# One of the four sums of x made by an accumulating transfer in a two-layer LoRA kernel

## The reference, cut to what matters

```python
base_out = jnp.einsum('bti,oi->bto', x, W) + b
lora_h = jnp.einsum('bti,bir->btr', x, A)
lora_out = jnp.einsum('btr,bro->bto', lora_h, Bm)
return base_out + lora_out * SCALING
...
x = x + _L0_cond_ref(x, itok_B_0_23, L0_cond_W, L0_cond_b, L0_cond_lora_As, L0_cond_lora_Bs)
x = x + _L1_cond_ref(x, itok_B_6_15, L1_cond_base_weight, L1_cond_base_bias, L1_cond_lora_A_w, L1_cond_lora_B_w)
```

## Time and profile before

| what | us |
|---|---|
| median of three runs (310.71 to 312.2) | 311.84 |
| the profiled execution, its own time | 312.06 |
| its span, first to last instruction | 310.5 |
| TensorE matmul, busy | 303.0 (98%) |
| VectorE, busy | 194.5 (63%) |
| ScalarE, busy | 90.3 (29%) |
| GpSimd, busy | 18.6 (6%) |

### The profile page before, as it was taken

How to read it: one execution, slowest core, us unless ns; L and a number is a source line. 1 busy time by engine, 2 the same in 40 slices (tenths; PEclk the granted TensorE clock), 3 DMA queues, 4 the chain that set the end, 5 groups by cost and what they waited for, 6 DMA issues and landing times.

```text
span 310.5 us, 4006 instructions
## 1 busy us (share of the span) xinstructions
PE 303.0 (98%) x1427; PEld 250.1 (81%) x1427; DVE 194.5 (63%) x328; ACT 90.3 (29%) x144; POOL 18.6 (6%) x43
## 2 busy tenths in 40 slices
PE   6999999999999999998999999999999999999995
PEld 4788898888887488886888888888888888888884
DVE  4777624994749362188897676487486485585312
ACT  4555534012122302293224223232231322232000
POOL 2233240000000010000000000000000000000000
PEclk9999999999999999999999999999999999999999
DMA  6996150000000055504054360440631711602002
GB/s 205 383 372 243 36 183 21 0 0 2 0 0 3 17 179 209 164 1 135 0 193 140 121 179 34 153 146 34 202 128 42 223 62 70 219 36 84 19 34 101
DMA packets 14744, 33.94 MB, mean 109 GB/s; under 512 B 2149, under 2 KB 2277, under 8 KB 14726
## 3 DMA queue, kind: packets, MB, share of 16 engines
q1 hardware_dynamic: 13702, 31.60, 30.0%
q0 software_dynamic: 1024, 2.10, 2.2%
HBM read 22.09 MB, written 11.60 MB: 109 GB/s over the span
## 4 chain that ended last, share of the span: by engine, by line
PE 91%; DVE 4%; ACT 2%; DMA 1%; SPq 0%; issue 0%
PE bank L807 28%; PE bank L921 16%; PE bank L920 16%; PE bank L922 16%; PE bank L940 4%; PE bank L819 3%; PE bank L927 2%; DMA stage<-W 1%; PE bank L895 1%; PE bank L897 1%; PE bank L896 1%; PE bank L821 1%; DVE w L602 1%; PE bank L868 1%; PE bank L906 1%; PE bank L907 1%
## 5 line engine op out<-in xcount | busy, mean ns | idle before, releaser
L807 PE MATMUL bank<-w,w_hi 128*128 128x512 f32 x256 | 80.9, 401 | 0.8 <-ACT w L350 0.6
L807 PEld LDWEIGHTS bank<-w,w_hi 128*128 128x128 f32 x256 | 49.2, 194 | 13.1 <-ACT w L350 1.3
L807 PE MATMUL bank<-w,w_lo 128*128 128x512 f32 x128 | 49.0, 390 | 0.0
L407 ACT CAST xa<-xr 128x512 fp32r<-128x512 f32 x32 | 19.6, 621 | 33.6 <-PE bank L927 17.3
L807 PEld LDWEIGHTS bank<-w,w_lo 128*128 128x128 f32 x128 | 24.1, 188 | 5.1
L921 PE MATMUL bank<-w_lo,w 128*128 128x512 f32 x64 | 25.1, 392 | 0.0
L922 PE MATMUL bank<-w_hi,w 128*128 128x512 f32 x64 | 25.1, 392 | 0.0
L920 PE MATMUL bank<-w_hi,w 128*128 128x512 f32 x64 | 25.0, 391 | 0.0
L921 PE MATMUL bank<-w 128*128 128x512 f32 x64 | 25.0, 391 | 0.0
L920 PE MATMUL bank<-w 128*128 128x512 f32 x64 | 25.0, 391 | 0.0
L920 PE MATMUL bank<-w_hi,xa 128*128 128x512 f32 x64 | 25.0, 390 | 0.0
(11 more groups left out here) (127 smaller groups left out, 493.4 us busy)
## 6 DMA issues: line engine op xcount, KB each, us to landing
xr<-xT SPq DMA_DIRECT2D x32, 256.0 KB, 4.2
out<-stage SPq DMA_DIRECT2D x28, 256.0 KB, 2.0
stage<-W SPq DMA_DIRECT2D x7, 512.0 KB, 5.0
stage<-W1T SPq DMA_DIRECT2D x7, 512.0 KB, 5.9
a<-rb_rows SPq DMA_DIRECT2D x8, 392.0 KB
rb_rows<-a SPq DMA_DIRECT2D x3, 512.0 KB
rb_rows<-b0w SPq DMA_DIRECT2D x3, 512.0 KB
out<-rows SPq DMA_DIRECT2D x4, 256.0 KB, 2.7
```

The lines of the kernel that those rows point to most:

```text
L407: nc.scalar.copy(x_op(j, 0), raw(j)).then_inc(op_hi[j], 1)
L807: return mm(d_bank(m, h)[:, :], left[:, m, k * P:(k + 1) * P], right[:, k, h * HALF:(h + 1) * HALF], start=start, stop=stop)
```

## The change

For batches 1 to 7 VectorE no longer makes S1. SyncE loads A21 a second time, straight into the tile of S1 (256 KB, right behind the ordinary load of A21), and GpSimd's queue then adds A22 from DRAM to it with an accumulating transfer (256 KB). ScalarE's `high_x(S1, b)` and VectorE's `sum_s2(b)` wait for that transfer (`s1_summed`) instead of VectorE's own sum. Batch 0 keeps the sum on VectorE. `load_a0(b)` for b from 2 on now alternates with the accumulating transfers on GpSimd's queue.

```diff
@@ load_x
-                        for s in {A11: (S2, S3), A21: (S1, S3), A12: (S4,), A22: (S1,)}[j]:
+                        for s in {A11: (S2, S3), A21: (S3,), A12: (S4,), A22: ()}[j]:
                             sp.wait_ge(s_made[s], b)
+                        if b == 1 and j in (A21, A22):
+                            sp.wait_ge(s_made[S1], 1)
                         if j in (A21, A12):
                             sp.wait_ge(op_lo[S3 if j == A21 else S4], b)
                     sp.dma_start(xr[:, j, :], xT[b, :, j, :]).then_inc(x_landed[j], DMA)
+                    if j == A21 and b >= 1:
+
+                        sp.wait_ge(op_lo[S1], b)
+                        sp.wait_ge(s_made[S2], b)
+                        sp.dma_start(s_raw[S1], xT[b, :, A21, :]).then_inc(s1_first, DMA)
@@ gpsimd
-            for b in range(2, B):
-                load_a0(b)
+            for b in range(1, B):
+                if b >= 2:
+                    load_a0(b)
+                pool.wait_ge(s1_first, b * DMA)
+                pool.dma_start(s_raw[S1], xT[b, :, A22, :], accum_op=ALU.add).then_inc(s1_summed, DMA)
@@ scalar, high_x
+                elif j == S1 and b >= 1:
+                    act.wait_ge(s1_summed, b * DMA)
@@ vector
             def sum_s1(b):
+                if b >= 1:
+                    return
                 dve.wait_ge(x_landed[A21], (b + 1) * DMA)
                 dve.wait_ge(x_landed[A22], (b + 1) * DMA)
-                if b >= 1:
-                    dve.wait_ge(op_lo[S1], b)
                 nc.vector.tensor_tensor(s_raw[S1], xr[:, A21, :], xr[:, A22, :], ALU.add).then_inc(s_made[S1], 1)
 
             def sum_s2(b):
...
-                dve.wait_ge(s_made[S1], b + 1)
+                if b >= 1:
+                    dve.wait_ge(s1_summed, b * DMA)
+                else:
+                    dve.wait_ge(s_made[S1], 1)
```

More of the change, by code:

```diff
@@ L180, in lora_pair @@
         op_lo = [sem(f"op_lo{j}") for j in range(8)]
+        s1_first = sem("s1_first")
+        s1_summed = sem("s1_summed")
         s_made = {j: sem(f"s_made{j}") for j in (S1, S2, S3, S4)}
```

## The result

The changed kernel takes 316.65 us (median of four, 315.62 to 318.16) against 311.64 us for the kernel before (median of four here, 310.71 to 312.2; its 311.84 above is of three of these), a ratio of 1.017 with a 95% interval of 1.011 to 1.0225. It is slower by 5.0 us; 3.1 of it is one wait of TensorE, in the place that was foretold. The trace is of the slowest of the four executions, 318.16 us.

The account below looks back on a forecast made before the run. TensorE, busy for 98% of the span, was taken as the bound. A 1.9 us stall in batch 2 and 0 us for all else, added to the median of 311.84, gave 313.7 us; range 311.2 to 320.7.

Parts of the forecast that it names:

- L: GpSimd's accumulating transfer, time from issue to landing: taken as 4.5 us, between 2.5 and 7.0 us.
- the sum: The forecast's addition over the batches: 1.9 us of TensorE stall in batch 2, 0 us elsewhere.
- the case that came true: The prediction's own case: L from 4.15 to 6.3 us, one stall in batch 2; chance 0.44.
- VectorE's relief: Batches 1 to 7: seven sums, 4.8 us busy time, leave VectorE; covered by TensorE's products, worth 0 us.
- Batch 2 is the tightest: Batch 2, prepared during batch 1: slack before TensorE needs u4 is 0.8 us, so it stalls 1.9 us.
- the hand-over: From the S1 copy's landing on SyncE to GpSimd's start of the accumulating transfer: taken as 0.3 us.
- rival 2: Slow transfer, L above 6.3 us: batches 3 to 7 stall too, 320.7 us at L = 7.0; chance 0.17.
- Rival 1: Quick transfer, L from 2.5 to 4.15 us: batch 2 stalls 0 to 1.55 us, no measurable change; chance 0.36.
- Now the S1 copy has this place: SyncE's loads in batch 2: the copy, third in order, issued at 160.5, lands 3.7 us later, at 164.2.
- the formula: Batch 2's stall: S2 starts at 164.6 + L, latest allowed 167.2, so TensorE waits L - 2.6 us.
- Batches 1 and 3 to 7: The chain fits up to L = 6.0 in batch 1 and 6.3 in batches 3 to 7: 0 us.
- The other loads at 0 us: SyncE's A12, A22 and factor loads and stores go 0.45 us later, their readers come later still: 0 us.

## Why the prediction was right, and where it was too small

The measured 316.65 us lies in the range (311.2 to 320.7) and on the forecast side; the forecast of 313.7 was 3 us too low. That the range holds it is in part luck: it was drawn so wide for an L of up to 7.0 us, L was 4.3, and what used up the room was not in the sum. The range of the case that came true, 313.4 to 315.8, was missed by 0.8 us.

- **VectorE's relief is worth nothing: right.** 5.8 us less busy time (foretold 4.8), no gain, also where the chain was harmless.
- **Batch 2 is the tightest, and `fill_z(1)` waits for u4: right**, in place and in number (once), but for 3.1 us in place of 1.9. With the start's 1.2 us taken off, the copy's issue (160.5), the hand-over (0.3 us), the 0.1 us to VectorE and the 4.6 us from S2 to u4 are those of the sum.
- **L = 4.5 us: near.** It was 4.3 us, well under rival 2's 6.3. Its terms came out as 3.5 us for the plain transfer in batch 2 (in the sum 3.6 + 0.2) and 0.8 us for the add (0.7), the latter from one execution of each kernel. Rival 1's bound of 4.15 us was only 0.1 us off: with the copy as foretold, the stall would have been 4.3 - 2.6 = 1.7 us, just above its 1.55. The estimate of 2.6 us from the Trainium skill, "DMA: Bandwidth & Descriptors", is under every transfer measured, with the add (4.0 to 5.0) or without (3.5 to 5.3).
- **"Now the S1 copy has this place", landing after 3.7 us: this is the step that failed.** I took the landing time of the load that had held third place. The copy needed 5.6 us, 1.9 more. The added load was priced as if it queued, not as something that changes the landing of those beside it; the runs show that its source being read twice and the load of A22 behind it both add, 0.9 us each, taken one at a time. With 5.6 and 4.3 the formula gives 160.5 + 5.6 + 0.3 + 4.3 + 0.1 - 167.2 = 3.6 us, the 3.5 us measured.
- **The clock was not in the sum.** 1.2 us of the loss is matmuls at the lower level behind the standstill. I had read a clock of full tenths in all slices and priced a stall by its length.
- **Batches 1 and 3 to 7: right, but barely for batch 3.** There the copy took 6.3 us and the transfer 5.0; the chain from the copy's issue to S2 was 6.3 + 0.3 + 5.0 + 0.1 = 11.7 us, where the sum leaves room for 189.2 - 177.6 = 11.6. `fill_z(2)`'s weight load waited 0.2 us and no matmul did, where 1.8 us had been foretold as left over. Batch 1's S2 waited 0.6 us on VectorE, covered.
- **The other loads at 0 us: nearly right.** The sum let only the loads behind the copy go later. But A21's load ahead of it landed 1.0 us later in batch 2 (4.3 us in place of 3.3 from issue), and the weight load behind u2 waited 0.3 us; the slack there hid all but 0.2 us.

## What to carry to other kernels

Work taken off an engine that isn't waited for is worth nothing, while the transfers that replace it must fit the slack of the tightest pass, which here was the first full one and not the average one. A transfer put among others in flight made them land later here, so neither its old neighbour's landing time nor an earlier start can be counted in full: hold back the transfers that nobody needs yet. A stall of TensorE of 2 to 3 us should be priced with something on top for the clock, here 1.2 to 1.5 us in five of seven traces.

## What was not expected of the hardware

- Loads in flight hold each other up: with a fifth 256 KB load and the accumulating transfer, the x loads' median from issue to landing went from 4.2 to 5.4 us; the accumulating transfer took 4.3 us behind the loads and 6.9 in the middle of them.
- Two loads of the same 256 KB, 0.4 us apart, landed after 4.3 and 5.6 us; with different sources after 3.6 and 4.7 us (batch 2, one execution each).
- After a standstill of 2.2 to 3.2 us TensorE was granted 0.50 for about 3 us in five profiled kernels, which cost 1.2 to 1.5 us, and stayed at 1.00 after one of 3.1 us and one of 2.3 us.
